# Explicit instruction lists for all eight tiles of a quantised attention and LoRA-expert kernel

## The reference

```
x: (2, 512, 1024), ctx: (2, 1024, 1024), all f32
fake_quant(v, s, z) = (clip(round(v / s + z), 0, 255) - z) * s
x = x + fake_quant(layernorm(x)) @ fake_quant(ctx)
y = layernorm(x)
logits = y @ gate_w.T                      # 8 experts, the two largest, softmax over them
base = y @ base_w.T + base_b
lora = sum over experts of w_full[e] * (y @ lora_A[e].T) @ lora_B[e].T      # rank 16
out = x + base + 2 * lora
```

## Time and profile before

| | us |
|---|---|
| median of 3 runs | 197.53 (196.81 to 198.03) |
| the profiled execution | 196.73 |
| its span, first to last instruction | 194.9 |
| TensorE busy | 170.9 (88%) |
| VectorE busy | 123.3 (63%) |
| ScalarE busy | 77.6 (40%) |
| mean granted TensorE clock | 0.982 |

### The profile page before, as it was taken

The page is one execution under the profiler, slowest core; times in us unless marked ns, Lnnn a source line. Parts: engine busy times, 40 slices in busy tenths (PEclk is TensorE's granted clock), DMA queues, the critical chain, the costliest instruction groups (busy, mean ns, idle before and its releaser), DMA issues.

```text
span 194.9 us, 2441 instructions
## 1 busy us (share of the span) xinstructions
PE 170.9 (88%) x862; PEld 123.3 (63%) x862; DVE 123.3 (63%) x314; ACT 77.6 (40%) x132; POOL 16.2 (8%) x33
## 2 busy tenths in 40 slices
PE   5837687959898998997888399999999999999993
PEld 2312243548686877885376276878688868888882
DVE  0688566889989969899403856765675506561521
ACT  2366949809247152756550412732243230110000
POOL 2022003201010000000041100110011000100000
PEclk9996999999999999999999789999999999999999
DMA  4999996999947520322019590425053500350112
GB/s 90 403 415 409 412 408 256 199 243 347 308 182 152 174 87 20 120 100 108 0 27 182 114 219 0 94 49 148 35 100 58 166 3 0 53 162 0 59 54 105
DMA packets 9515, 29.55 MB, mean 152 GB/s; under 512 B 1184, under 2 KB 1184, under 8 KB 9504
## 3 DMA queue, kind: packets, MB, share of 16 engines
q1 hardware_dynamic: 7344, 22.06, 30.3%
q0 software_dynamic: 2016, 7.34, 20.3%
q10 hardware_dynamic: 144, 0.00, 0.0%
HBM read 22.05 MB, written 4.19 MB: 135 GB/s over the span
## 4 chain that ended last, share of the span: by engine, by line
PE 56%; DVE 23%; ACT 10%; DMA 5%; issue 5%; SPq 0%; DVEq 0%; ACTq 0%
PE ps_odd L837 17%; PE ps_even L837 16%; PE ps_att L795 6%; PE ps_g L829 3%; PE ps_t L779 3%; DMA x_sb<-zfix 2%; DMA x_sb<-in_x 2%; DVE stats L515 2%; DVE x_sb L568 2%; DVE yt L593 2%; DVE stats L511 2%; DVE c L557 2%; ACT zfix L365 1%; DVE w_lo L599 1%; ACT qx L337 1%
## 5 line engine op out<-in xcount | busy, mean ns | idle before, releaser
L837 PE MATMUL ps_even<-w_hi,yt 128*128 128x512 f32 x128 | 38.0, 403 | 0.8 <-ACT zfix L365 0.8
L837 PE MATMUL ps_odd<-w_hi,yt 128*128 128x512 f32 x128 | 36.7, 400 | 0.0
L837 PEld LDWEIGHTS ps_even<-w_hi,yt 128*128 128x128 f32 x128 | 23.7, 192 | 5.6 <-issue 1.0
L795 PE MATMUL ps_att<-c,c1t 128*128 128x512 f16 x96 | 23.9, 389 | 2.3 <-ACT c1t L344 2.3
L837 PEld LDWEIGHTS ps_odd<-w_hi,yt 128*128 128x128 f32 x128 | 22.8, 188 | 4.2
L385 ACT ACTIVATE yt<-ps_t 128x512 fp32r<-128x512 f32 x15 | 9.0, 597 | 33.2 <-PE ps_t L779 33.2
L837 PE MATMUL ps_even<-w_lo,yt 128*128 128x512 f32 x64 | 20.9, 403 | 0.0
L593 DVE TENSOR_TENSOR yt<-ps_t,yt 128x512 fp32r<-128x512 f32 x15 | 10.4, 690 | 15.1 <-ACT yt L385 14.9
L319 ACT ACTIVATE ln_v<-mv,eps 128x1 f32<-128x1 f32 x16 | 4.7, 293 | 37.8 <-DVE mv L516 37.8
L829 PE MATMUL ps_g<-ag,yt 128*128 128x272 f32 x64 | 17.2, 343 | 2.1 <-DVE yt L593 2.1
L837 PE MATMUL ps_odd<-w_lo,yt 128*128 128x512 f32 x64 | 18.7, 392 | 0.0
(11 more groups left out here) (99 smaller groups left out, 252.8 us busy)
## 6 DMA issues: line engine op xcount, KB each, us to landing
ring<-in_ctx SPq DMA_DIRECT2D x12, 512.0 KB, 10.1
w_raw<-in_w_t SPq DMA_DIRECT2D x8, 512.0 KB, 15.5
x_sb<-in_base_b POOLq DMA_DIRECT2D x8, 512.0 KB, 5.4
out_x<-x_sb SPq DMA_DIRECT2D x16, 256.0 KB, 2.5
x_sb<-in_x SPq DMA_DIRECT2D x7, 512.0 KB, 6.5
x_sb<-zfix POOLq DMA_DIRECT2D x6, 512.0 KB, 5.4
x_sb<-in_ctx SPq DMA_DIRECT2D x4, 512.0 KB, 7.9
ag_raw<-in_ag_t SPq DMA_DIRECT2D x1, 544.0 KB, 14.1
```

The source lines that it names most:

```text
L795: ins = pe.matmul(att_bank(t)[h][:, :], c1t[:, t % 4, k, :], c2[:, k, h * HALF:(h + 1) * HALF], start=(k == 0), stop=(k == CT - 1))
L837: pe.matmul(ffn_bank[t % 2][h][:, :], rows_of(part, t, k), w[:, k, h * HALF:(h + 1) * HALF], start=start, stop=False)
```

## The change

All four lists are written out to tile 7. SP: x1 ahead of the first context tile, contexts 8 and 9 among the weights, x4 and x5 behind the weights, x6, x7 and contexts 13 to 15 between the stores. VectorE: `quant_constants` first, x scalars and cuts in another order. TensorE: attention of batch 0 in another order; `base` is three functions: `base_high` (both passes with `w_hi`, waits for its rows and its weight slice), `base_low` (the pass with `w_lo`) and `base` (all three); attention slices of tiles 4 to 7 stand singly or in small groups between base slices; tile 7's two halves are interleaved with the end of tile 6. Waits are added: `low_and_gate(t)` for t of 2 and more and `transpose_low(t)` for t of 1 and more wait for `ltlo_ready`, `top_logits` for `loww_ready`, `cut_context` of batch 1 for `colsum_psum`, ScalarE's first `split_y_hi(1, .)` for `ag_ready`. `stats` gets a place for each tile. The work of each engine, in number and size of instructions, is the same, but for these waits. Ahead of the orders stands the diff of loads, waits and functions; the three order lists follow as the calls of their new side, several to a line, a loop in brackets.

```diff
-        stats = sb("stats", [P, 2, 2, 6], F32)
+        stats = sb("stats", [P, 2, TILES, 2, 6], F32)
...
             load_x(0)
+            load_x(1)
             load_context(0)
-            load_x(1)
             load_context(1)
+            load_x(2)
             load_context(2)
-            load_x(2)
             load_context(3)
-            load_context(4)
             load_x(3)
-            for k in range(5, CT):
+            for k in range(4, 9):
                 load_context(k)
-            sp.dma_start(ag_raw[:, :], ag_t).then_inc(ag_in, 16)
-            for k in range(KT):
-                sp.dma_start(w_raw[:, k, :], w_d[k]).then_inc(w_in[k], 16)
-            sp.dma_start(b_raw[:, :], b_t).then_inc(b_in, 16)
-            for t in range(TPB, TILES):
-                load_x(t)
-            for k in range(CT, 2 * CT):
+            load_w(0)
+            load_w(1)
+            load_ag()
+            load_w(2)
+            load_context(9)
+            for k in range(3, 8):
+                load_w(k)
+            load_x(4)
+            load_x(5)
+            for k in range(10, 13):
                 load_context(k)
-            for t in range(TILES):
-                for h in range(2):
-                    cols = slice(h * HALF, (h + 1) * HALF)
-                    sp.wait_ge(out_ready, 2 * t + h + 1)
-                    sp.dma_start(out_d[t][:, cols], x_sb[:, t, cols]).then_inc(stored, 16)
+            load_b()
+            store(0, 0)
+            store(0, 1)
+            load_x(6)
+            load_x(7)
+            for k in range(13, 16):
+                load_context(k)
+            store(1, 0)
+            store(1, 1)
...
+            store(7, 0)
+            store(7, 1)
             sp.wait_ge(stored, 32 * TILES)
...
                 act.wait_ge(yt_psum, 2 * t + g + 1)
                 if t >= 2:
                     act.wait_ge(ffn_done, t - 1)
+                if t == 1:
+
+                    act.wait_ge(ag_ready, 1)
                 act.activation(yt[:, t % 2, 0, 4 * g:4 * g + 4, :].rearrange("p k m -> p (k m)"), y_bank(t, g)[:, :],
                                ACT.Copy).then_inc(yhi_ready, 1)
 
...
                 context_scaled(dve, k)
                 if k >= CT:
                     dve.wait_ge(att_done, TPB)
+                    dve.wait_ge(colsum_psum, 1)
                 dve.tensor_scalar(c2[:, k % CT, :], qc[:, k % QSLOTS, :], QMAX, -CENTRE,
                                   ALU.min, ALU.add).then_inc(c2_ready, 1)
 
...
 
             def top_logits(t):
                 dve.wait_ge(ag_done, t + 1)
+                if t >= 1:
+                    dve.wait_ge(loww_ready, t)
                 chain(dve.tensor_copy(low_g[:, :], ps_g[:, 0:AG]))
                 chain(dve.tensor_tensor(low_g[:, :], low_g[:, :], ps_g[:, AG:2 * AG], ALU.add))
...
                 if t == 0:
                     pe.wait_ge(ag_ready, 1)
                     pe.wait_ge(ylo_ready, 2)
+                elif t == 1:
+                    pe.wait_ge(top_ready, 1)
                 else:
-                    pe.wait_ge(top_ready, t)
+                    pe.wait_ge(ltlo_ready, t)
                 for k in range(KT):
                     if t >= 1 and k % 4 == 0:
                         pe.wait_ge(ylo_ready, 2 * t + k // 4 + 1)
...
                     if k < KT - 1:
                         pe.matmul(ps_g[:, 0:AG], l, ag[:, k, 0, :], start=False, stop=False)
                 ins.then_inc(ag_done, 1)
-
-            def base(t, k, part, w, halves=(0, 1), start=False):
-                for h in halves:
-                    pe.matmul(ffn_bank[t % 2][h][:, :], rows_of(part, t, k), w[:, k, h * HALF:(h + 1) * HALF],
-                              start=start, stop=False)
 
             def bank_free(t):
                 if t == 0:
...
                     if t == 3:
                         pe.wait_ge(zfix_ready, 4)
 
+            def one_pass(t, k, part, w, halves, start):
+                for h in halves:
+                    pe.matmul(ffn_bank[t % 2][h][:, :], rows_of(part, t, k), w[:, k, h * HALF:(h + 1) * HALF],
+                              start=start, stop=False)
+
+            def base_high(t, k):
+                if k == 0:
+                    bank_free(t)
+                if k % 4 == 0:
+                    pe.wait_ge(ylo_ready, 2 * t + k // 4 + 1)
+                pe.wait_ge(whi_ready, k + 1)
+                one_pass(t, k, 0, w_hi, (0, 1), k == 0)
+                one_pass(t, k, 1, w_hi, (0, 1), False)
+
+            def base_low(t, k):
+                pe.wait_ge(wlo_ready, k + 1)
+                one_pass(t, k, 0, w_lo, (0, 1), False)
+
+            def base(t, k, halves=(0, 1)):
+                if k == 0:
+                    bank_free(t)
+                if k % 4 == 0:
+                    pe.wait_ge(ylo_ready, 2 * t + k // 4 + 1)
+                one_pass(t, k, 0, w_hi, halves, k == 0)
+                one_pass(t, k, 0, w_lo, halves, False)
+                one_pass(t, k, 1, w_hi, halves, False)
+
             def transpose_low(t):
                 pe.wait_ge(loww_ready, t + 1)
                 if t == 0:
 
                     pe.wait_ge(top_ready, 2)
+                else:
+                    pe.wait_ge(ltlo_ready, t)
                 pe.transpose(low_t, low_w[:, :], ident_f[:, :]).then_inc(lowt_psum, 1)
 
             def lora(t, h):
...
                 ins.then_inc(ffn_done if h else ffn_half, 1)
```

More of the change, by code:

```diff
@@ L698, in _ @@
             split_low_lo(0)
[L699 to L709 removed]
+            split_w_lo(6)
+            split_b_lo()
+            cut_context(9)
+            sum_context(1)
+            split_w_lo(7)
+            variance(0, 4)
@@ new lines, in _ @@
+            low_and_gate(3)
+            for k in range(0, 7):
+                base(3, k)
+            transpose_c1(5)
+            base(3, 7)
+            attention(5, 0)
+            transpose_y(4, 0)
+            for k in range(1, 7):
+                attention(5, k)
+            transpose_y(4, 1)
+            for k in range(0, 4):
+                base(4, k)
+            transpose_low(3)
+            attention(5, 7)
+            transpose_c1(6)
+            base(4, 4)
+            base(4, 5)
@@ new lines, in _ @@
+            low_and_gate(4)
+            lora(3, 0)
+            lora(3, 1)
+            attention(6, 0)
+            attention(6, 1)
+            base(4, 6)
+            transpose_y(5, 0)
+            attention(6, 2)
+            attention(6, 3)
+            base(4, 7)
+            attention(6, 4)
+            transpose_low(4)
+            for k in range(5, 8):
+                attention(6, k)
+            transpose_y(5, 1)
+            for k in range(0, 3):
+                base(5, k)
+            transpose_c1(7)
@@ new lines, in _ @@
+            base(5, 3)
+            low_and_gate(5)
+            attention(7, 0)
+            lora(4, 0)
+            lora(4, 1)
+            transpose_y(6, 0)
+            attention(7, 1)
+            base(5, 4)
+            base(5, 5)
+            transpose_y(6, 1)
+            attention(7, 2)
+            attention(7, 3)
+            transpose_low(5)
+            for k in range(4, 7):
+                attention(7, k)
+            base(5, 6)
+            base(5, 7)
+            lora(5, 0)
+            lora(5, 1)
@@ new lines, in _ @@
+            attention(7, 7)
+            low_and_gate(6)
+            for k in range(0, 4):
+                base(6, k)
+            transpose_low(6)
+            transpose_y(7, 0)
+            base(6, 4)
+            base(6, 5)
+            base(7, 0, (1,))
+            transpose_y(7, 1)
+            base(6, 6)
+            base(6, 7)
+            for k in range(1, 4):
+                base(7, k, (1,))
+            low_and_gate(7)
+            base(7, 4, (1,))
+            base(7, 5, (1,))
+            base(7, 0, (0,))
```

476 lines of the change are left out of this document (271 added, 205 removed).

## The result

The changed kernel takes 180.0 us (median of 4, 179.72 to 183.74), beside 197.78 for the kernel before in the same series: 0.911 of its time, 95% interval 0.906 to 0.916. 181.1 was forecast, in a range of 178.5 to 189. The profiled execution took 179.92 with a span of 178.0, 16.9 less than before. Executions more than 1.5% longer than the fastest of their kernel, such as the one of 183.74, are left out of every ratio here, and since the profiled ones of experiments 2 and 5 are of that kind, only their waits are read.

The account below looks back on a forecast made before the run. TensorE, busy 170.9 of 194.9 us, was taken as the bound. 101.1 + 72.6 + 0.7 (changes) + 1.0 (slips) gave the last matmul at 175.4; 3.15 more the span, 178.5; plus 2.6, 181.1 us; range 178.5 to 189.

Parts of the forecast that it names:

- Where the time was: TensorE loses 24.9 us: 17.8 of waits, half-clock stretches and matmul tails; the gain comes only from these and the start.
- The leads: TensorE ahead of the kernel before: 6.1 us at low_and_gate(0), 8.2 at tile 1's end, 10.4 at low_and_gate(3).
- tight points: Places in tiles 0 and 1 where results come barely in time: split_y_lo(1, 1), base_low(0, 7) waiting 0.4, base(2, 4) 0.3.
- The half clock: First batch: TensorE at half clock for about 4 us behind its wait, costs some 2 us, and catches up.
- the rival that the half clock holds: First batch: TensorE at 1.2 GHz until tile 0's y at 36 us; no gain or slower, 196 to 200; chance 0.06.
- The changes between f16 and f32: Tiles 4 to 7: some 14 more changes between f16 attention and f32 base, 0 to 1.3 us, taken as 0.7.
- the slips (1.0): Allowance of 1.0 us for slower context cuts beside a GpSimd scaling and other small slips.
- Tiles 4 to 7: the lists are worth nothing.: TensorE is full there and no VectorE or ScalarE result comes late, so the work is only reordered.
- The hole: Before tile 4: TensorE's 4.1 us wait for y and half-clock restart go; y at 98.0, asked for at 100.6, slack 2.6.
- New waits for weights: Rival: part of the gain stays in new waits, as zfix accumulates and weights slow each other; 185 to 191, chance 0.20.
- signs named for being wrong: Second half-clock stretch, TensorE over 2 us for yt, w_lo or y (35 to 100), ScalarE waiting for w_raw, transpose_y(4, 0) behind 104.
- The start: Reordered VectorE start: loss of 2.0 us on the first transpose (12.3) and 0.9 on attention (14.5).

Follow-up runs that it names:

- experiment 2: As Experiment 1, but in tile 3's loop tile 4's two y transposes stand behind the eighth base slice and six attention slices; 183.95 us, 0.932.
- experiment 5: Changed kernel with low_and_gate(0) put back in front of the first four base_high slices of tile 0; 182.52 us, 0.925.
- Experiment 1: Changed kernel with the lists of ScalarE, VectorE and TensorE from low_and_gate(3) on put back into the old loops; 185.95 us, 0.9455.
- experiment 6: Changed kernel with 12 more throw-away matmuls ahead of the first c1 transpose and 6 behind it; 182.59 us, 0.928.
- experiment 3: As experiment 2, with VectorE's top_logits(3) and weigh_low(3) ahead of add_attention(4), exp_gate(3) ahead of first_guess(1, 4), lora(3) behind attention 5; 182.16 us, 0.923.
- experiment 4: Kernel before with only tile 4's two y transposes moved behind tile 3's eighth base slice and six attention slices; 195.12 us, 0.986.
- experiment 9: Changed kernel with the start of VectorE's order as in the kernel before; 180.07 us, 0.912.
- experiment 11: As experiment 6, with context 9 and load_b loaded directly behind the weights; 179.23 us, 0.908.

## Why the prediction was right, and where it wasn't

Its steps beside the changed kernel's trace:

| step | predicted | measured |
|---|---|---|
| first transpose; attention | 12.3; 14.5 | 11.61; 14.01 |
| attention of tile 0 done | 25.4 | 25.93 |
| `base_high(0, 0)` | 35.9 | 36.83 |
| `low_and_gate(0)`, lead | 39.7, 6.1 | 40.68, 5.1 |
| tile 1 ends, lead | 76.5, 8.2 | 77.03, 7.7 |
| `low_and_gate(3)`, lead | 86.8, 10.4 | 87.11, 10.1 |
| y of tile 4 made; asked for | 98.0; 100.6 | 98.9; 101.1 |
| `transpose_y(4, 0)` done | 101.1 | 101.70 |
| from there to the last matmul's end | 74.3 | 73.1 |
| last matmul ends | 175.4 | 174.8 |
| span; what lies around it | 178.5; 2.6 | 178.0; 2.0 |

- **Where the time was.** Right for the waits: no work was removed, and 13.1 of the 16.9 us are waits. The clock, which the prediction counts among the sources, gave next to nothing in sum: 7.0 us at 1.2 GHz before, 6.8 after. Experiment 1 shows some 11 us to be the front's and 6.0 the late lists', and experiment 5 shows 2.5 of the front's 11 at their place. Which of the front's other edits brought the rest (the order of the loads, the cuts, the split of `base`) was not taken apart.
- **The leads.** Right within 1.0 us, and later within 0.5, since the tight points around the weights gave no wait at all.
- **The half clock.** "Costs some 2 us, and catches up" was wrong in its second half, and the stretch was longer than taken: from attention's start at 14.01 to about 19.4, 5.4 us and not 4, which costs 2.7. TensorE did not catch up: VectorE waited 1.46 for tile 0's attention, and experiment 6 reaches y of tile 0 1.5 us sooner without it. The walk had the end of that attention 0.5 too early (25.4, measured 25.93), over half of the 0.9 us by which the front was late. As the rival that the half clock holds it did not come: the clock was 1.00 from 20 us on, through all small gaps and changes of kind. The Trainium skill (TensorE: Matmul & The Clock Gate, "A second HAM failure mode") tells of small pauses that made the clock go up and down in another kernel; no such swing shows here behind 20 us, where the only wait left is 0.70.
- **The changes between f16 and f32.** Taken at 0.05 each (0.7 in all), but 12 base matmuls behind attention take 2.75 in the chain above, against 2.73: 0.02 a change. Only behind c1 transposes are they 2.81, as in the earlier trace rows. With the slips (1.0), of which a part had shown already ahead of 101 us, this term was 1.2 too large. It hid the 0.6 that `transpose_y(4, 0)` was late, and the margin around the span was 0.6 less. So the total is closer than its terms: small errors of both signs cancelled, and that is luck.
- **"Tiles 4 to 7: the lists are worth nothing."** Wrong by 1.4 to 2.0 us: experiment 3 has late waits for `lt_lo` and y there that the written-out lists avoid. I looked only for late results in the new lists, not for those that the old loops would have with TensorE 10 us ahead.
- **The hole.** Right in time (slack 2.2 us, predicted 2.6), but its price was told only as TensorE's 4.1 and the clock. Experiments 2 and 4 show two further waits that come when TensorE's transposes alone are moved (0.8 to 1.3, and 1.6, half of the 5.8); the new VectorE list keeps them away.
- **New waits for weights.** I gave this rival 0.20 and took the last slice at 40 to 41. It was used by ScalarE at 41.48 in the changed kernel, with a wait of 0.57 that stayed hidden, as did one of 3.37 for `b_raw` at 53.80. ScalarE waiting for `w_raw` was one of the signs named for being wrong, so this rival was near. Experiment 6 is this rival as it would have been: 1.5 us sooner in front, 2 us later at the end. The prediction was right with less room than its chance says.
- **The start** was taken as a loss of 0.9 on attention; it is 0.4, and experiment 9 shows none of it to be the list's order.

Open: why experiment 11's runs scatter above its profiled one, what the 0.3 and 0.6 us not found in experiments 1 and 3 are, and how the front's 11 us divide.

## What to carry to other kernels

When the bound engine is idle in the middle of a kernel, fill it with independent work held back for that place, and move every engine's list together: a wait closed in one list alone came back here, by half, as the next in-order waits of another. Price the fill by the prices of uninterrupted pieces of the chain, since that is what a full engine runs at. And before making a front stage faster, look at which transfers it starts: here the accumulates, started sooner, cost more than the clock had gained. Putting them behind the weights, or the loads that are needed later behind those needed sooner, kept the gain.
